# A fused feed-forward, recurrence, feed-forward kernel on 8 cores: gate projections and scans at other places, one product moved into layer one, weight sums all on VectorE, two more plain tiles

## The chip, the cores and the metric

One Trainium2 chip (trn2), 8 cores, each with its own two sequences of the batch of 16; the cores don't talk to each other. The metric is the device time in microseconds of the slowest core. Three runs of the kernel before took 4605.74, 4753.08 and 4896.73 us; their median, 4753.08 us, is its time.

## The reference

```python
# x: (16, 4096, 1024) f32;  w1: (4096, 1024), w2: (1024, 4096), Wa, Wx: (1024, 1024)
def ffn(x):                     # twice: before and after the recurrence
    h = gelu(bitlinear(x, w1, b1))          # exact gelu
    return bitlinear(h, w2, b2)
def bitlinear(x, w, b):
    x = x * rsqrt(mean(x*x) + 1e-5)
    xq = round(x * 127/max|x|) * max|x|/127      # 8-bit activations per token
    wq = clip(round(w / mean|w|), -1, 1) * mean|w|   # ternary weights
    return xq @ wq.T + b
def recurrence(x):
    r, i = sigmoid(x @ Wa.T + ba), sigmoid(x @ Wx.T + bx)
    a = exp(-8 * softplus(-Lam) * r)
    h[t] = a[t] * h[t-1] + sqrt(1 - a*a)[t] * (i * x)[t]
    return h
x = x + 0.5 * ffn(layernorm(x))
x = x + recurrence(layernorm(x))
x = x + 0.5 * ffn(layernorm(x))
```

## The kernel before

Tokens are worked on in tiles of 128. A core has 64 tiles, and each passes the feed-forward twice, so that there are 128 **slots** `j`, one tile each: `plan` (L316) mixes tiles of the first pass with tiles of the second. The recurrence works on groups `t` of 256 tokens; its work is cut into steps (`recur`, L967) laid into three slots in a row for each group. With `R0 = 9`, slot j has stage (j - 9) % 3.

**Setup** (`weights`, L142) loads w1 and w2, finds their mean absolute values, rounds and clips them to ternary fp8 numbers and transposes them. It ends near 172 us. w2T, the ternary w2, stays in SBUF until slot 6; then its room is used by the recurrence.

**One slot**, as the loop at L1089 writes it, in the order of the queues (each engine works strictly in the order in which the loop issues to it, and waits only for semaphores):

- layer one in four parts: `mm1(cur, p)` is 16 matmuls of 512 columns on TensorE into one of two PSUM buffers `f_pm`; `evict1` is the VectorE pass that takes it to SBUF (L498) and the gelu on ScalarE (L504); `gmax` is the VectorE maximum (L509).
- between the parts, for the next tile: `stats`, `centre` (VectorE L426, then the GpSimd addition L429) and `quant1` (from L434 on). For the tile before: `t2`, two times 8 transposes on TensorE into one of two PSUM buffers `aux` and a copy of 1.85 us on ScalarE (L469).
- then `scale2`, and rows 0 to 3 (`row`, L1073), between which the next tile's `t1` (4 transposes), the quantising of the hidden layer (`quant2`), squares on ScalarE and the steps of the recurrence stand.

**Layer two.** For two tiles (slots 2K and 2K+1) it takes seven products of 16 matmuls in place of eight (a scheme of the Strassen kind): `product(K, o)` for o = 0 to 6. Their right sides are sums of quarters of w2, kept in DRAM as `w2x` and read back piece by piece, 512 KB each, into four buffers `w_x`; a piece is asked for when the piece four earlier is used up (`w2_piece`, L621). Their left sides are sums that VectorE makes (`sum1` to `sum4`, L694 to L716) in even slots. Slots with even j hold three products, odd ones four. The first pair (slots 1 and 2) is worked plainly from w2T (`mm2`, L568), 64 matmuls a tile.

**Making w2x**: `w2_plain` stores three quarters as they are; `w2_sum` (L737) makes four sums, in four parts each (u = j = 0 to 3), steps 0 and 2 on VectorE, steps 1 and 3 on GpSimd; `w2_stage` stores them. All four steps of a part stand at the end of the slot, and the first `product` is in slot 4. In slots 1 to 4, `gate_piece` (L780) transposes the gate weights.

**The recurrence of a group**: stage 0 brings in the normalised input by transposes (`g_tr_in`); stage 1 has the gates of channels 0 to 3 and stage 2 those of channels 4 to 7 (`g_gate`: 16 matmuls of 256 columns into `aux`, two tanh on ScalarE, the gate's weights loaded into one of three buffers). Half 0's `g_decay` and `g_root` (exp, square, square root on ScalarE, L901 to L915) stand at the end of stage 1, half 1's at the end of stage 2. `g_gated` (VectorE L918), `g_product` (L925) and `g_scan` (L929, four scans of 256 and a copy) follow in layer one of the next slot; `g_tr_out` (L944) is four transposes of the result into `aux` and an addition by VectorE (L956), which frees the buffer. The two for half 1 stand in stage 0 of the next group: the first straight after layer one (at = -1), the second after row 0 and `t1` (at = 0).

**`aux`** has two buffers, taken strictly in turn (`next_aux`, L383) by `t2`, `t1`, `g_tr_in`, `g_gate` and `g_tr_out`. Whoever writes one waits for the reader of its last content.

All loads and stores go through SyncE's queue, in order.

Of the kernel before, what the change touches and what calls it, by code (L numbers as in the profile page):

```python
# [88 lines left out]
def build_program(B_core=2, S_seq=4096):  # L89
# [34 lines left out]
    with ExitStack() as top:  # L124
# [189 lines left out]
        R0 = 9  # L314

# [22 lines left out]
        def stream_phase():  # L338
# [13 lines left out]
            with ExitStack() as ph:  # L352
# [11 lines left out]
                with nc.Block("stream") as blk:  # L364
# [250 lines left out]
                    n_pieces = 14 * (len(tiles) // 2 - 1)  # L615
# [12 lines left out]
                    def product(K, o):  # L628
# [7 lines left out]
                        for half in range(2):  # L636
                            i = 14 * (K - 1) + 2 * o + half
# [99 lines left out]
                    def w2_sum(u, step):  # L737
# [5 lines left out]
                        eng = ("vector", "gpsimd", "vector", "gpsimd")[step]  # L743
# [5 lines left out]
                            eng, lambda e: e.tensor_tensor(  # L749
# [217 lines left out]
                    def recur(j, at):  # L967
# [12 lines left out]
                        if stage == 0:  # L980
                            if 1 <= t <= NG:
                                if at == -3:
                                    g_gated(t - 1, 1)
                                    g_product(t - 1, 1)
                                elif at == -2:
                                    g_scan(t - 1, 1)
                                elif at in (-1, 0):
                                    g_tr_out(t - 1, at + 1, 1)
# [11 lines left out]
                        elif stage == 1:  # L1000
                            if live and -1 <= at < 3:
                                g_gate(t, at + 1)
                            if live and at == 3:
# [6 lines left out]
                        elif live:  # L1010
                            if at == -3:
                                g_gated(t, 0)
                                g_product(t, 0)
                            elif at == -2:
                                g_scan(t, 0)
                            elif at < 3:
                                g_gate(t, at + 5)
                                if at in (1, 2):
                                    g_tr_out(t, at - 1, 0)
                            else:  # L1020
# [52 lines left out]
                    def row(j, r):  # L1073

                        K = j // 2 - 1
                        if j in (1, 2):
                            mm2(j - 1, r)
                        elif j >= 4 and (j % 2 == 1 or r < 3):
                            product(K, r + 3 * (j % 2))

                    def row_out(j, r):
                        K = j // 2 - 1
                        if j in (1, 2):
                            if r == 3:
                                outp(j - 1)
                        elif j >= 4 and (j % 2 == 1 or r < 3):
                            product_out(K, r + 3 * (j % 2))

                    for j in range(len(slots) + 2):  # L1089
                        cur, nxt, pre = tile(j), tile(j + 1), tile(j - 1)  # L1090
                        K = j // 2 - 1
                        even = j % 2 == 0 and j >= 4
                        order = (1, 0) if j % 2 == 0 else (0, 1)
                        if j == 6:
                            sch.fence([gate_prep[k] for k in ("cast15", "tr15", "wg14", "wg15")]
                                      + [prep["x2"], prep["x3"], prep["plain"], T[1]["mm2"]])
# [130 lines left out]
```

How the kernel before makes its waits and increments, by code:

```python
            def body(engine, ops=ops):  # L73
                passed = {}
                for waits, fn, sem, n in ops:
                    for s, v in waits:
                        if passed.get(s, 0) >= v:
                            continue
                        engine.wait_ge(self.sems[s], v)
                        passed[s] = v
                    ins = fn(engine)
                    if n:
                        ins.then_inc(self.sems[sem], n)
# [1096 lines left out]
            @blk.sync  # L1180
            def _(q):
                for s in ("sOA", "sOB", "sGO"):
                    q.wait_ge(sch.sems[s], sch.count[s])
                q.nop()
```

## Time and profile before

| what | before |
|---|---|
| median of 3 runs | 4753.08 us (4605.74 to 4896.73) |
| the profiled execution | 4604.44 us |
| its span on the slowest core | 4602.9 us; the others 4574.7 to 4602.9 |
| busy | TensorE 4191.7 us (91%), VectorE 3457.2 (75%), ScalarE 2778.1 (60%), GpSimd 935.6 (20%) |
| granted TensorE clock, mean | 0.971 |
| DMA | 864.66 MB, 188 GB/s, 54.8% of the 16 engines; a piece of `w_x` or a gate's weights (512 KB) lands 5.4 us after its issue |
| eviction of a product (L668), `g_norm` (L843) | 0.75 and 0.80 us, mean |

A row of a time order has the start in us from the span's beginning, the duration in us, the engine, the line of the kernel and the instruction, output<-input with the shapes, and how many there were; in brackets is how long the engine was idle before it and what ended that. The end of a matmul is modelled and reaches into the next one. A granted clock of 1 is 2.4 GHz, of 0.5 it is 1.2 GHz.

### The profile page before, as it was taken

Reading aid. Unit: us, or ns where it says so; the run is one execution under the profiler, and the core shown is the slowest. Engines: PE = TensorE matmul, PEld = TensorE weight load, DVE = VectorE, ACT = ScalarE, POOL = GpSimd, SP = SyncE. Lnnn points to the kernel's source line nnn. Section 1 sums busy time; section 2 is a strip of 40 time slices with the busy share of each in tenths; the row PEclk is TensorE's granted clock in tenths of the full one; section 3 lists DMA queues with packets and bytes.
Section 4 is the critical chain, followed back from the end, with each engine's and each line's share of the span. In section 5 each row is a group of like instructions: output and inputs, shape, how many; then the busy total and the mean of one; then the engine's idle time right before and its main releaser. Section 6 shows DMA issues by size and latency. Waiting matters only on the chain.

```text
span 4602.9 us, 72256 instructions; the slowest of 8 cores (4574.7 to 4602.9 us)
## 1 busy us (share of the span) xinstructions
PE 4191.7 (91%) x23447; PEld 2225.5 (48%) x23447; DVE 3457.2 (75%) x4616; ACT 2778.1 (60%) x3464; POOL 935.6 (20%) x1549
## 2 busy tenths in 40 slices
PE   1679999999999999999999999999999999999999
PEld 0334544555555555555554555555555555444444
DVE  4777787777778777777787777778777777777775
ACT  4544666666666666666666666666666666555443
POOL 0232121212212122111121112212212111222221
PEclk9989999999999999999999999999999999999999
DMA  9455545555555555556555555555555555455545
GB/s 286 158 181 166 203 170 188 175 200 200 190 188 190 202 198 175 188 189 209 192 175 188 176 194 203 192 188 195 203 197 170 193 182 192 149 178 179 169 166 179
DMA packets 243090, 864.66 MB, mean 188 GB/s; under 512 B 25608, under 2 KB 31904, under 8 KB 242592
## 3 DMA queue, kind: packets, MB, share of 16 engines
q1 hardware_dynamic: 242720, 860.04, 54.8%
q8 instruction: 193, 3.16, 0.3%
q14 instruction: 177, 1.45, 0.1%
HBM read 747.75 MB, written 112.20 MB: 187 GB/s over the span
## 4 chain that ended last, share of the span: by engine, by line
PE 76%; DVE 10%; DMA 7%; issue 5%; SPq 1%; ACT 1%; POOL 0%; DVEq 0%; ACTq 0%; POOLq 0%
PE f_po L641 31%; PE f_pm L485 30%; PE aux L876 10%; DMA w_x<-w2x 6%; PE aux L462 2%; DVE f_h L498 2%; DVE w2T L934 2%; DVE f_col L509 2%; PE aux L948 2%; DMA p_ring<-L_ffn_w 2%; SPq L62 1%; DVE f_col L434 1%; DVE w2T L918 1%; PE aux L852 1%; PE f_po L574 1%
## 5 line engine op out<-in xcount | busy, mean ns | idle before, releaser
L485 PE MATMUL f_pm<-w1T,f_q1T 128*128 128x512 fp8e4 x8192 | 1840.0, 380 | 15.6 <-DVE f_h L498 10.6
L485 PEld LDWEIGHTS f_pm<-w1T,f_q1T 128*128 128x128 f16 x8192 | 792.9, 98 | 918.4 <-issue 29.3
L641 PE MATMUL f_po<-w_x,f_A 128*128 128x512 fp8e4 x5040 | 1182.7, 390 | 54.1 <-DMA w_x<-w2x 51.1
L504 ACT ACTIVATE f_h<-f_h 128x1024 f32<-128x1024 f32 x512 | 537.7, 1056 | 820.6 <-DVE f_h L498 811.5
L498 DVE SCALAR_TENSOR_TENSOR f_h<-f_pm,f_col,f_b1c 128x1024 f32<-128x1024 f32 x512 | 654.8, 1279 | 252.4 <-PE f_pm L485 247.2
L668 DVE SCALAR_TENSOR_TENSOR f_xb<-f_po,f_col,f_xb 128x512 f32<-128x512 f32 x504 | 376.7, 749 | 619.7 <-PE f_po L641 592.4
L641 PEld LDWEIGHTS f_po<-w_x,f_A 128*128 128x128 f16 x5040 | 501.4, 100 | 632.1 <-issue 127.2
L509 DVE TENSOR_REDUCE f_col<-f_h 128x1 f32<-128x1024 f32 x512 | 616.3, 1214 | 14.5 <-ACT f_h L504 5.3
L516 ACT ACTIVATE f_sqj<-f_h 128x1024 bf16<-128x1024 f32 x512 | 540.6, 1056 | 26.6 <-ACT f_sqj L516 0.7
L429 POOL TENSOR_TENSOR f_xb<-f_xb,f_b2c 128x1024 f32<-128x1024 f32 x128 | 302.2, 2361 | 1053.0 <-DVE f_xb L426 1011.6
L641 PE MATMUL f_po<-w_x,f_s 128*128 128x512 fp8e4 x2016 | 493.6, 401 | 10.3 <-DMA w_x<-w2x 8.7
L876 PE MATMUL aux<-w2T,g_w 128*128 128x256 bf16 x4096 | 488.9, 273 | 0.3 <-ACT w2T L890 0.3
L469 ACT CAST f_A<-aux 128x2048 f16<-128x2048 int8 x256 | 472.8, 1847 | 16.5 <-PE aux L462 16.5
L876 PEld LDWEIGHTS aux<-w2T,g_w 128*128 128x128 bf16 x4096 | 397.6, 98 | 87.4 <-issue 0.4
L545 POOL TENSOR_TENSOR f_col<-f_col 128x2 f32<-128x2 f32 x128 | 36.9, 289 | 1798.4 <-ACT f_sqj L516 1798.4
L469 ACT CAST f_q1T<-aux 128x1024 f16<-128x1024 int8 x128 | 129.6, 1012 | 392.4 <-PE aux L462 392.4
L641 PEld LDWEIGHTS f_po<-w_x,f_s 128*128 128x128 f16 x2016 | 206.9, 103 | 257.3 <-issue 63.0
L886 ACT ACTIVATE w2T<-aux,ba_h 128x256 f32<-128x256 f32 x256 | 120.6, 471 | 329.1 <-PE aux L876 329.1
L539 DVE TENSOR_SCALAR f_q<-f_h,f_col 128x1024 int8<-128x1024 f32 x448 | 305.8, 742 | 0.1
L948 PE MATMUL aux<-ident_f,w2T 128*128 128x128 f32 x512 | 92.6, 312 | 177.5 <-DVE w2T L934 166.7
L462 PEld LDWEIGHTS aux<-ident_b,f_q 128*128 128x128 bf16 x2560 | 175.2, 98 | 96.2 <-issue 6.1
L462 PE MATMUL aux<-ident_b,f_q 128*128 128x128 bf16 x2560 | 205.6, 219 | 6.0 <-ACT f_q L443 6.0
(103 smaller groups left out, 3718.5 us busy)
## 6 DMA issues: line engine op xcount, KB each, us to landing
w_x<-w2x SPq DMA_DIRECT2D x882, 512.0 KB, 5.4
g_w<-wg SPq DMA_DIRECT2D x256, 512.0 KB, 5.4
p_ring<-L_ffn_w SPq DMA_DIRECT2D x64, 512.0 KB, 16.1
f_xb<-L_attn_x SPq DMA_DIRECT2D x64, 512.0 KB, 6.2
xs<-f_xb SPq DMA_DIRECT2D x64, 512.0 KB, 5.9
g_xg<-xs SPq DMA_DIRECT2D x32, 1024.0 KB, 8.7
xs<-g_xg SPq DMA_DIRECT2D x32, 1024.0 KB, 7.4
f_xb<-xs SPq DMA_DIRECT2D x64, 512.0 KB, 5.7
```

Of the source, the lines that this page charges most:

```text
L429: tj["xb2"] = put("gpsimd", lambda g: g.tensor_tensor(x[:], x[:], b2c[:], op=ALU.add), waits=tok_b2 + [tj["xc"]])
L462: a = put("tensor", lambda t, c=c: t.transpose(out[:, c * 128:(c + 1) * 128], words[:, c * 128:(c + 1) * 128], ident_b[:]), waits=(waits_p ...
L469: ev = put("scalar", lambda s: s.copy(dst.rearrange("p (c i t) -> p c i t", i=2, t=128), pair), waits=[a] + waits_act)
L485: a = put("tensor", lambda t, k=k, hf=hf, o=o: t.matmul(pm[i][:, hf * 512:(hf + 1) * 512], q1T[:, k * 128:(k + 1) * 128], w1T[:, o:o + 512 ...
L498: ev = put("vector", lambda v: v.scalar_tensor_tensor(hg[:, sl], pm[i][:], col(n, C1), b1c[:, sl], op0=ALU.mult, op1=ALU.add), waits=[tj[" ...
L504: tj["gelu%d" % p] = put("scalar", lambda s: s.activation(hg[:, sl], hg[:, sl], AF.Gelu), waits=[ev])
L509: T[n]["gm"] = put("vector", lambda v: v.reduce_max(col(n, GM + p), hg[:, sl], axis=AX.X, apply_absolute_value=True), waits=[T[n]["gelu%d" ...
L516: tj["sq"] = put("scalar", lambda s: s.activation(sqj[:], hg[:, sl], AF.Square, accum_out=col(n, SQ + p)), waits=[tj["gelu%d" % p], tj.get ...
L539: T[n]["q2"] = T[n]["q2_%d" % (p // 2)] = put("vector", lambda v: v.tensor_single_scalar(q2[:, sl], hg[:, sl], col(n, S2), op=ALU.mult), w ...
L641: a = put("tensor", lambda t, k=k, c=c, w=w: t.matmul(po[:, bank * 512:(bank + 1) * 512], lhs[:, k * 128:(k + 1) * 128], w[:, c * 512:(c + ...
L668: "vector", lambda v: v.scalar_tensor_tensor(x[:, sl], po[:, bank * 512:(bank + 1) * 512], col(n, C2), x[:, sl], op0=ALU.mult, op1=ALU.add),
L876: a = put("tensor", lambda q, h=h, k=k: q.matmul(aux[i][:, h * TW:(h + 1) * TW], w[:, h * D + k * 128:h * D + (k + 1) * 128], xnB[:, k * T ...
```

## The change

There are five edits.

1. `PLAIN = 4`: four tiles (slots 1 to 4) instead of two are worked plainly from w2T; products begin in slot 6.
2. `w2_sum` runs on VectorE alone, one step after each row of slots 0 to 3; the stores follow row 3. The first loads of `w_x` are asked for at the end of slot 4.
3. Product 3 of a pair, the one from `sum1`, moves in odd slots from row 0 to the middle of layer one, between parts 1 and 2; the other three are rows 0 to 2. There is no row 3 after slot 5.
4. Two gates stand right behind layer one (at = -1), the third at 0 and the fourth at 1; `g_decay` and `g_root` move from 3 to 2, ahead of row 3's place.
5. `g_gated` moves to the very start of the slot (at = -5, ahead of `evict1(cur, 0)`), `g_product` behind `evict1(cur, 1)` (-4), `g_scan` behind `quant1` (-3), ahead of `gmax(cur, 0)` and `evict1(cur, 2)`. The places of `g_tr_out` for half 1 stay.

```diff
+        PLAIN = 4
...
-                    n_pieces = 14 * (len(tiles) // 2 - 1)
+                    n_pieces = 14 * (len(tiles) // 2 - PLAIN // 2)
...
-                            i = 14 * (K - 1) + 2 * o + half
+                            i = 14 * (K - PLAIN // 2) + 2 * o + half
...
-                        eng = ("vector", "gpsimd", "vector", "gpsimd")[step]
...
-                            eng, lambda e: e.tensor_tensor(
+                            "vector", lambda v: v.tensor_tensor(
...
                         if stage == 0:
                             if 1 <= t <= NG:
-                                if at == -3:
+                                if at == -5:
                                     g_gated(t - 1, 1)
+                                elif at == -4:
                                     g_product(t - 1, 1)
-                                elif at == -2:
+                                elif at == -3:
                                     g_scan(t - 1, 1)
...
                         elif stage == 1:
-                            if live and -1 <= at < 3:
-                                g_gate(t, at + 1)
-                            if live and at == 3:
+                            if live and at == -1:
+                                g_gate(t, 0)
+                                g_gate(t, 1)
+                            if live and at in (0, 1):
+                                g_gate(t, at + 2)
+                            if live and at == 2:
                                 g_decay(t, 0)
                                 g_root(t, 0)
...
                         elif live:
-                            if at == -3:
+                            if at == -5:
                                 g_gated(t, 0)
+                            elif at == -4:
                                 g_product(t, 0)
-                            elif at == -2:
+                            elif at == -3:
                                 g_scan(t, 0)
-                            elif at < 3:
-                                g_gate(t, at + 5)
-                                if at in (1, 2):
-                                    g_tr_out(t, at - 1, 0)
-                            else:
+                            elif at == -1:
+                                g_gate(t, 4)
+                                g_gate(t, 5)
+                            elif at == 0:
+                                g_gate(t, 6)
+                            elif at == 1:
+                                g_gate(t, 7)
+                                g_tr_out(t, 0, 0)
+                            elif at == 2:
+                                g_tr_out(t, 1, 0)
                                 g_decay(t, 1)
                                 g_root(t, 1)
...
-                        if j in (1, 2):
+                        if 1 <= j <= PLAIN:
                             mm2(j - 1, r)
-                        elif j >= 4 and (j % 2 == 1 or r < 3):
-                            product(K, r + 3 * (j % 2))
+                        elif j >= PLAIN + 2 and r < 3:
+                            product(j // 2 - 1, r + 4 * (j % 2))
...
+                        if j < 4:
+                            w2_sum(j, r)
+                            if r == 3:
+                                for step in range(4):
+                                    w2_stage(j, step)
...
+                        recur(j, -5)
                         if cur is not None:
                             mm1(cur, 0)
                             evict1(cur, 0)
...
                             mm1(cur, 1)
                             evict1(cur, 1)
+                        recur(j, -4)
                         if pre is not None:
                             t2(pre, order[0])
                         if nxt is not None:
                             quant1(nxt)
+                        recur(j, -3)
+                        if odd:
+                            product(K, 3)
                         if cur is not None:
                             gmax(cur, 0)
                             mm1(cur, 2)
-                            recur(j, -3)
                             evict1(cur, 2)
+                        if odd:
+                            product_out(K, 3)
+                        if cur is not None:
                             gmax(cur, 1)
                         if pre is not None:
                             t2(pre, order[1])
                         if cur is not None:
                             mm1(cur, 3)
                             evict1(cur, 3)
-                            recur(j, -2)
                             gmax(cur, 2)
                             gmax(cur, 3)
                             scale2(cur)
                         recur(j, -1)
...
-                        if j < 4:
-                            for step in range(4):
-                                w2_sum(j, step)
-                            for step in range(4):
-                                w2_stage(j, step)
-                        if j == 3:
+                        if j == 4:
                             wx_ready += [sch.tok(x) for x in XSEM + ("sXP",)]
```

Here `even` and `odd` are true from slot 6 on, for even and odd j.

## Rows read from the trace of the kernel before

**Rows 1.** Waits of TensorE, whole span (total us, times, longest us).

```profile
PE aux L948 <- DVE w2T L934: 166.7, 30, 5.9
PE f_po L641 <- DMA w_x<-w2x: 59.8, 46, 5.7
```

**Rows 2.** TensorE from 2081.75 (start, duration us, instructions, [idle before]).

```profile
2081.75 7.07 PE L485 MATMUL f_pm<-w1T,f_q1T 128*128 128x512 fp8e4 x32
2093.01 3.62 PE L485 MATMUL f_pm<-w1T,f_q1T 128*128 128x512 fp8e4 x16
2102.15 1.09 PE L948 MATMUL aux<-ident_f,w2T 128*128 128x128 f32 x4 [5.53 <-DVE w2T L934]
2103.03 5.67 PE L641 MATMUL f_po<-w_x,f_A 128*128 128x512 fp8e4 x16
2132.56 1.91 PE L876 MATMUL aux<-w2T,g_w 128*128 128x256 bf16 x16
```

**Rows 3.** VectorE in time order, same slot, and the sums at its end.

```profile
2085.61 1.28 DVE L498 SCALAR_TENSOR_TENSOR f_h<-f_pm,f_col,f_b1c 128x1024 f32<-128x1024 f32 x1 [1.98 <-PE f_pm L485]
2090.44 1.21 DVE L434 TENSOR_REDUCE f_col<-f_xb 128x1 f32<-128x1024 f32 x1
2092.11 1.22 DVE L509 TENSOR_REDUCE f_col<-f_h 128x1 f32<-128x1024 f32 x1
2093.25 1.22 DVE L918 SCALAR_TENSOR_TENSOR w2T<-w2T 128x1024 f32<-128x1024 f32 x1
2094.57 1.23 DVE L925 TENSOR_TENSOR w2T<-w2T 128x1024 f32<-128x1024 f32 x1
2095.71 1.28 DVE L498 SCALAR_TENSOR_TENSOR f_h<-f_pm,f_col,f_b1c 128x1024 f32<-128x1024 f32 x1
2099.22 2.67 DVE L934 TENSOR_TENSOR_SCAN w2T<-w2T,carry 128x256 f32<-128x256 f32 x4
2105.18 0.69 DVE L956 TENSOR_TENSOR g_xg<-aux,g_xg 128x512 f32<-128x512 f32 x1
2117.98 1.22 DVE L708 TENSOR_TENSOR f_A<-f_s,f_A 128x2048 f16<-128x2048 f16 x1
```

**Rows 4.** ScalarE in time order, same slot.

```profile
2084.93 1.06 ACT L914 ACTIVATE w2T<-w2T 128x1024 f32<-128x1024 f32 x1
2097.08 1.06 ACT L504 ACTIVATE f_h<-f_h 128x1024 f32<-128x1024 f32 x1 [2.60 <-DVE f_h L498]
2098.05 1.85 ACT L469 CAST f_A<-aux 128x2048 f16<-128x2048 int8 x1
2099.79 1.06 ACT L504 ACTIVATE f_h<-f_h 128x1024 f32<-128x1024 f32 x1
```

**Rows 5.** GpSimd in time order: the same slot, and slot 1's end.

```profile
2089.48 2.37 POOL L429 TENSOR_TENSOR f_xb<-f_xb,f_b2c 128x1024 f32<-128x1024 f32 x1 [11.27 <-DVE f_xb L426]
...
236.22 3.83 POOL L749 TENSOR_TENSOR w_x<-w2T 128x2048 fp8e4<-128x2048 fp8e4 x1 [5.75 <-DVE w_x L749]
```

**Rows 6.** VectorE in time order, around 236 us.

```profile
233.79 2.28 DVE L749 TENSOR_TENSOR w_x<-w2T 128x2048 fp8e4<-128x2048 fp8e4 x1
236.25 5.94 DVE L749 TENSOR_TENSOR w_x<-w_x,w2T 128x2048 fp8e4<-128x2048 fp8e4 x1 [0.17 <-DVE w_x L749]
```

**Rows 7.** TensorE in time order, around the first slots' waits.

```profile
243.53 5.26 PE L485 MATMUL f_pm<-w1T,f_q1T 128*128 128x512 fp8e4 x16 [3.92 <-DVE f_h L498]
254.95 3.61 PE L574 MATMUL f_po<-w2T,f_A 128*128 128x512 fp8e4 x16 [2.26 <-ACT f_A L469]
324.53 5.72 PE L641 MATMUL f_po<-w_x,f_A 128*128 128x512 fp8e4 x16 [5.74 <-DMA w_x<-w2x]
```

**Rows 8.** Busy time by engine in a stretch, with TensorE granted clock (PEclk).

```profile
172.00:377.00 205.00, 164.85 (x856) 78.41 (x857) 151.04 (x168) 98.72 (x112) 72.25 (x74) 0.92 0.50 162
```

**Rows 9.** Waits of TensorE between 640 and 4100, then 4100 and 4603 us.

```profile
PE f_po L641 <- DMA w_x<-w2x: 29.4, 21, 2.7
...
PE f_po L641 <- DMA w_x<-w2x: 13.9, 16, 1.7
```

More of the change, by code:

```diff
@@ L1073, in row @@
                     def row(j, r):
-                        K = j // 2 - 1
-                        if j in (1, 2):
+                        if 1 <= j <= PLAIN:
                             mm2(j - 1, r)
-                        elif j >= 4 and (j % 2 == 1 or r < 3):
-                            product(K, r + 3 * (j % 2))
+                        elif j >= PLAIN + 2 and r < 3:
+                            product(j // 2 - 1, r + 4 * (j % 2))
                     def row_out(j, r):
-                        K = j // 2 - 1
-                        if j in (1, 2):
+                        if 1 <= j <= PLAIN:
                             if r == 3:
                                 outp(j - 1)
-                        elif j >= 4 and (j % 2 == 1 or r < 3):
-                            product_out(K, r + 3 * (j % 2))
+                        elif j >= PLAIN + 2 and r < 3:
+                            product_out(j // 2 - 1, r + 4 * (j % 2))
+                        if j < 4:
[3 more added lines that the diff above has]
+                                    w2_stage(j, step)
                     for j in range(len(slots) + 2):
@@ L1091, in stream_phase @@
                         K = j // 2 - 1
-                        even = j % 2 == 0 and j >= 4
+                        even = j % 2 == 0 and j >= PLAIN + 2
+                        odd = j % 2 == 1 and j >= PLAIN + 2
                         order = (1, 0) if j % 2 == 0 else (0, 1)
@@ L1095, in stream_phase @@
                             sch.fence([gate_prep[k] for k in ("cast15", "tr15", "wg14", "wg15")]
-                                      + [prep["x2"], prep["x3"], prep["plain"], T[1]["mm2"]])
-                        if cur is None and even:
+                                      + [prep["x2"], prep["x3"], prep["plain"],
+                                         T[PLAIN - 1]["mm2"]])
+                        drain = cur is None and even
+                        if drain:
                             for r in range(2):
@@ L1129, in stream_phase @@
                         recur(j, -1)
-                        if cur is not None or not even:
+                        if not drain:
                             row(j, 0)
@@ L1145, in stream_phase @@
                             sum3(K)
-                        if cur is not None or not even:
+                        if not drain:
                             row(j, 1)
```

## The prediction

> **What bounds the kernel.** I read the waits of TensorE first, then its instructions in order of time, then the other engines in the same slot. TensorE is busy 91% of the span and in most slots has no gap at all. Its largest wait, 166.7 us in 30 places, is `g_tr_out` waiting for the scans; the pieces `w_x` cost 59.8 us in 46 [rows 1]. Below, S is a slot's first matmul; the slot at S = 2081.75 is even, with stage 0. Layer one ends, and TensorE stands 5.53 us until the scans of half 1 are through, because they stand behind `evict1(cur, 3)`. What follows is slow: the four transposes take 1.09 us and the next product 5.67 where 16 such matmuls take 3.62 [rows 2], the granted clock being at its lower level. That wait costs about 5.5 + 0.5 + 2.05 = 8.1 us, so a pair of groups (six slots: one even and one odd slot of each stage) pays 16.1, and 16 such pairs pay 258 us. This is what edits 4 and 5 aim at. The question is whether VectorE and `aux` let it go.
>
> **The new place of the scans (edit 5).** TensorE without gaps: 16 matmuls are 7.07 - 3.62 = 3.45 us, a gate 1.91 less the same 0.17 of overlap, 1.74 [rows 2]; with two `t2` of about 0.45, layer one ends at S + 14.7, and in an odd slot, which now has a product in its middle, at S + 18.2. VectorE is anchored to TensorE by the first eviction at S + 3.86 (2085.61) and then works without a break. In before, L434 starts at S + 8.69, `gmax` at 10.36, `g_gated` 11.50, `g_product` 12.82, the third eviction at 13.96 [rows 3]. Now `g_gated` lies under TensorE's first part, and `g_product` stands ahead of L434, at S + 8.69. It reads two SBUF tensors while GpSimd's L429 runs, S + 7.73 to 10.10 [rows 5]. No row has these two together, since L925 came 4 us later. The nearest is L749: 5.94 us when a GpSimd L749 had begun just before, against 2.28 for its twin [rows 6]: it waited until GpSimd was done. The price of this collision lies between 0 and 2.37 us; I take 1.4, the end of L429 less the start of `g_product`, as in the L749 row. Then L434 starts at 11.2, the scans at 12.9 (quant1's 1.67 us later), `gmax` at 15.8 (2.67 and a copy) and the third eviction at 16.9, 3.0 us later than in before.
>
> The Trainium skill (SBUF — State Buffer, "Who interferes with whom") says that a VectorE instruction with two SBUF inputs and a GpSimd instruction that reads SBUF exclude each other, the later one waiting for the whole of the first. The L749 rows agree (5.94 us against 2.28). Without that rule the sum below would be 4541 us.
>
> **Who is late next.** `t2`'s second copy on ScalarE stands behind the gelu of part 2, so it starts when the third eviction is through: before, at S + 16.3 until 18.15 [rows 4]; now until 21.1. It holds one `aux` buffer. The gelu of part 3 follows it, then `gmax(cur, 3)` at 22.1, `scale2`, and the addition L956 of the first `g_tr_out` at 24.05 to 24.7, which holds the other. From this:
> - *stage 0, even*: the scans are ready 15.8, TensorE is there at 14.7; `t1` finds `aux` free at 21.3; the second `g_tr_out` starts at 25.0 where without waits it would at 18.8. **6.2 us** in three steps, in place of 5.53.
> - *stage 2, even*: the second of the two gates behind layer one needs the buffer of the `t2` copy: free at 21.3, wanted at 14.7 + 1.74 = 16.45: **4.85 us**. This is new: before, one gate stood there.
> - *odd slots*: TensorE comes 3.45 us later, but VectorE begins the slot with `sum2` and `sum4` (1.22 each [rows 3]) of the even slot before, and `g_gated` now stands ahead of the first eviction. Counted from the end of product 2, with a start after 0.34, an eviction of 0.7, the sums' 2.4, `g_norm`'s 0.75 and `g_gated`'s 1.15: 5.3 against 3.86, shift 1.5, in stage 2; 0.9 in stage 0. Stage 2: free at 22.9, wanted 19.9, **3.0 us**. Stage 0: with product 3's own eviction (0.66) as well, free at 26.0, wanted 22.3, **3.7 us**.
> - *stage 1*: no scan; the copy is through at about S + 15.8 and the second gate comes at 16.45: nothing. The root is done in time: it ended at S + 4.24 in the slot [rows 4] and moves by less than a row of 3.45, to 7.7 at most, ahead of 8.69.
>
> Waits for six slots: 17.75 us, before 11.06. **Clock**: a wait of 2.26 us was followed by full speed (16 matmuls in 3.61), one of 3.92 by 5.26 [rows 7], one of 5.53 by 2.54 us of loss in all. I take 2.5 for the 6.2, 1.9 for the 4.85, 1.7 for the 3.7, and for the 3.0, between 0 and 1.64, the middle, 0.8: 6.9. In all 24.6 against 16.1: +8.5 for six slots, times 16 = **+136 us**.
>
> **Product 3 inside layer one (edit 3).** Same matmuls, and `sum1` and its pieces are long there. Its two pieces are given back earlier, so the four `w_x` buffers refill under layer one. In before the pieces made TensorE wait 29.4 us between 640 and 4100 us, at 2.7 us at the most [rows 9]; the new waits give the loads time as well. I take 20 us of it back (0 to 30). Where products follow each other without gates, behind 3940 us, the waits are short and many (13.9 us in 16 from 4100 on [rows 9]); only odd slots, with four products in a row, can run through four buffers that way, and now none has more than three: I take 15 (8 to 18). SyncE's queue keeps its order of waits; the gate weights, two asked for in quick succession, have about 12 us until their use, against 5.4 for a landing.
>
> **The first slots (edits 1 and 2).** The stretch from slot 0 to slot 6 lasts 205.0 us, of which TensorE is busy 164.9 at 0.92 of the clock [rows 8]. A slot with plain rows and gate pieces is 30.5 us of TensorE. Now: slot 0 19; slot 1 about 42 (VectorE's sums, 4 x 2.28 us in place of two, push its evictions by some 4 us, partly taken out of a wait that was there); slots 2 and 3 about 33.3 each (16 sums cost 36.5 us of VectorE against 25.6 before, but they lie beside the rows; the block ahead of the first eviction, 2.28 + 5.94, which gave the 3.92 us wait [rows 6, 7], is gone); slot 4 31; slot 5, with no layer two, 19.5. Sum 178: **-26 us** (-10 to -35). Two more plain tiles are 16 matmuls more, 3.45 us, contained in this. The wait for the first piece, 5.74 us and its slow product [rows 7], goes, since the pieces are now asked for a slot ahead. Of the 59.8 us of piece waits, 29.4, 13.9 and this 5.7 leave 10.8 for slots 4 to 9 and around 4000 us; I take **-8** for slots 6 to 9 (0 to -10).
>
> **Sum** against the profiled execution: 4604.4 + 136 - 20 - 15 - 26 - 8 = 4671, say **4670 us**, +1.4%. The profiled execution stands 149 us below the median of the three runs shown; I keep to it as the base, and let the range reach up. A difference under 2%, 4512 to 4697, is about what can't be told from no change.
>
> **Rivals.**
> 1. *The wait just goes* (0.12). If the copy and the addition come earlier than I place them, TensorE has no gap in stages 0 and 2: 4604 - 258 - 69 = 4277 us. For: VectorE is idle for a quarter of the span. Against: the idle time lies in stage 1 and late in the slots, and the copy stands behind a later eviction by order.
> 2. *No collision with GpSimd* (0.20). Each of the four waits is 1.4 us shorter: 4.8, 3.45, 1.6 and 2.3, 12.1 in all, with 4.4 of clock 16.5 for six slots, nearly before's 16.1: 4604 + 6 - 69 = 4541. For: L925 always took 1.22 to 1.23 us. Against: it never stood beside L429.
> 3. *Slower: the clock* (0.18). Place: every slot of stages 0 and 2. Price: the 2.54 us that followed the wait of 5.53 [rows 2], after each of the four waits: 17.75 + 10.2 = 27.9 against 16.1, + 189, so 4604 + 189 - 69 = 4724. It decides if waits of 3 to 4 us in quick succession always bring the lower level; 3.92 did, 2.26 didn't.
> 4. *Mine* (0.50): 4600 to 4740.
>
> The change does what it says on every engine; the only part that may not act is the shorter time for pieces.
>
> **Range**: 4520 to 4790. Below it takes in most of rival 2, above it rival 3 and part of the spread of the runs shown; rival 1 is left out. Faster by over 2%: rival 1 and a third of rival 2, 0.18. Slower by over 2%: most of rival 3 and the upper quarter of mine, 0.28. Within: 0.54.
>
> **What would show it.** Right: no wait of `g_tr_out` beyond about 1 us for the scans, but waits of TensorE for ScalarE's L469 (gate at L876 and `t1`) and for VectorE's L956, 3 to 6 us in every slot of stages 0 and 2; L925 at 2.6 us; third evictions at S + 17; no piece waits in the tail; slot 6 starting near 351 us instead of 377. Wrong: L925 at 1.23 (rival 2); waits under 1 us at gates and `g_tr_out` (rival 1); a mean granted clock clearly under 0.97 (rival 3); or a VectorE backlog that makes `mm1` wait for evictions, which I have at nothing because `f_pm` is next needed in the following slot.

## The result and the profile after

The changed kernel's profiled execution took 4652.14 us against 4604.44, +1.0%. Against runs of the kernel before on the same chip (4603.36 us at best) the ratio is 1.011, 95% interval 1.0065 to 1.0152: slower, by less than the 2% that the prediction called hard to tell from no change. The four runs took 4652.14, 4656.47, 4883.84 and 4968.73 us; in the two long ones the cores of one die show a lower granted clock, as happens in some executions of every version here, so that ratios and not medians are compared below. The span is 4650.6 us on the slowest core, the mean granted clock 0.964 (0.971 before), TensorE is busy 4226.9 us and VectorE 3528.9.

What makes TensorE wait has changed hands. Waits of TensorE over the whole span, changed kernel: total us, times, longest us. Lines between 316 and 740 have a number one higher than before (L470 was L469, L642 was L641); L876 to L956 keep theirs.

```profile
PE aux L876 <- ACT f_A L470: 110.7, 33, 4.8
PE aux L948 <- DVE g_xg L956: 109.2, 32, 3.6
PE aux L463 <- ACT f_A L470: 21.2, 16, 1.3
PE aux L948 <- DVE w2T L934: 11.3, 15, 0.8
PE f_po L642 <- DMA w_x<-w2x: 9.2, 16, 1.4
```

[Rows 1] had 166.7 us in 30 for the scans and 59.8 in 46 for pieces. The scans' wait is down to 11.3, and 241 us of waits for the copy and the addition that free an `aux` buffer have come (110.7 + 109.2 + 21.2), none of which were there. All of the 9.2 us for pieces lies behind 3985 us.

The same even slot of stage 0 as in [rows 2], TensorE in time order (start, duration us, instructions, idle before):

```profile
2103.22 0.63 PE L948 MATMUL aux<-ident_f,w2T 128*128 128x128 f32 x4 [0.78 <-DVE w2T L934]
...
2108.63 0.38 PE L463 MATMUL aux<-ident_b,f_q 128*128 128x128 bf16 x4 [1.33 <-ACT f_A L470]
2112.33 1.09 PE L948 MATMUL aux<-ident_f,w2T 128*128 128x128 f32 x4 [3.32 <-DVE g_xg L956]
2113.21 5.53 PE L642 MATMUL f_po<-w_x,f_A 128*128 128x512 fp8e4 x16
```

One wait of 5.53 us has become three, 0.78, 1.33 and 3.32, in all 5.43; and the slow product behind them, at the lower of the two clock levels for most of its time, is still there (5.53 us for what takes 3.62).

The next slots of stages 2 and 0, TensorE in time order: even stage 2 (layer one from 2159.50), odd stage 0 (from 2199.53), odd stage 2 (from 2268.53).

```profile
2180.48 3.57 PE L876 MATMUL aux<-w2T,g_w 128*128 128x256 bf16 x16 [4.37 <-ACT f_A L470]
2183.85 4.35 PE L642 MATMUL f_po<-w_x,f_A 128*128 128x512 fp8e4 x16
...
2225.45 0.63 PE L948 MATMUL aux<-ident_f,w2T 128*128 128x128 f32 x4 [3.48 <-DVE g_xg L956]
2225.91 5.30 PE L642 MATMUL f_po<-w_x,f_s 128*128 128x512 fp8e4 x16
...
2290.80 3.28 PE L876 MATMUL aux<-w2T,g_w 128*128 128x256 bf16 x16 [2.20 <-ACT f_A L470]
2293.88 3.96 PE L642 MATMUL f_po<-w_x,f_A 128*128 128x512 fp8e4 x16
```

The reason stands in the other queues of the even stage-2 slot. VectorE, then GpSimd, then ScalarE, in time order:

```profile
2168.12 2.47 DVE L925 TENSOR_TENSOR w2T<-w2T 128x1024 f32<-128x1024 f32 x1
2172.16 2.66 DVE L934 TENSOR_TENSOR_SCAN w2T<-w2T,carry 128x256 f32<-128x256 f32 x4
2176.16 1.28 DVE L499 SCALAR_TENSOR_TENSOR f_h<-f_pm,f_col,f_b1c 128x1024 f32<-128x1024 f32 x1
...
2167.15 2.35 POOL L430 TENSOR_TENSOR f_xb<-f_xb,f_b2c 128x1024 f32<-128x1024 f32 x1 [3.87 <-DVE f_xb L427]
...
2177.53 1.06 ACT L505 ACTIVATE f_h<-f_h 128x1024 f32<-128x1024 f32 x1 [4.05 <-DVE f_h L499]
2178.49 1.85 ACT L470 CAST f_A<-aux 128x2048 f16<-128x2048 int8 x1
2180.24 1.06 ACT L505 ACTIVATE f_h<-f_h 128x1024 f32<-128x1024 f32 x1
```

The product L925 takes 2.47 us where it took 1.23 [rows 3], since GpSimd's L430 runs at the time. The third eviction starts 16.66 us into the slot (S + 13.96 before), ScalarE stands 4.05 us for it, and its copy, behind the gelu, frees TensorE's buffer at 2180.3; the gate starts at 2180.48, 4.37 us after TensorE had come to it.

Busy time by engine in four stretches (from the setup's end to slot 6, to slot 10, to the drain, to the end), with the granted clock as the third number from the end:

```profile
172.00:348.00 176.00, 157.41 (x873) 76.32 (x874) 144.78 (x162) 95.14 (x105) 45.87 (x60) 0.98 0.50 156
348.00:460.00 112.00, 111.87 (x576) 53.22 (x577) 92.10 (x125) 63.72 (x75) 27.85 (x48) 0.98 0.50 157
460.00:3996.00 3536.00, 3284.92 (x18504) 1787.40 (x18502) 2701.46 (x3563) 2218.30 (x2804) 755.76 (x1180) 0.95 0.56 185
3996.00:4651.00 655.00, 633.37 (x3249) 297.12 (x3246) 490.30 (x637) 322.92 (x363) 138.12 (x243) 1.00 0.52 176
```

Slot 6 starts at 347.96 (377.18 before), slot 10 at 460.07 (497.46), the first slot after the last scans at 4009.67 (3955.02). So 37.4 us are gained until slot 10, 92.0 are lost in the 96 slots behind it, and 7.0 are gained in the tail: together +47.7, the difference of the spans (4650.6 and 4602.9).

### The profile page after: what moved, and what is told of

It is laid out like the page before. It is cut to its first block, busy times and chain, and to the rows that moved or that the text cites. A ratio compares the mean times of both kernels' runs of the same rounds, so it can differ in the third digit from the quotient of the medians.

```text
span 4650.6 us, 72145 instructions; the slowest of 8 cores (4639.2 to 4650.6 us)
## 1 busy us (share of the span) xinstructions
PE 4226.9 (91%) x23463; PEld 2238.2 (48%) x23463; DVE 3528.9 (76%) x4614; ACT 2789.5 (60%) x3464; POOL 974.2 (21%) x1541
## 4 chain that ended last, share of the span: by engine, by line
PE 67%; DVE 17%; issue 7%; DMA 4%; ACT 3%; SPq 1%; DVEq 0%; POOL 0%; ACTq 0%; POOLq 0%
PE f_pm L486 28%; PE f_po L642 26%; PE aux L876 9%; DVE f_h L499 3%; DVE w2T L934 2%; DVE w2T L925 2%; PE aux L463 2%; DMA w_x<-w2x 2%; ACT f_A L470 2%; DMA p_ring<-L_ffn_w 2%; PE aux L948 1%; DVE f_col L510 1%; PE aux L852 1%; DVE f_q L540 1%; SPq L62 1%
## 5 line engine op out<-in xcount | busy, mean ns | idle before, releaser
L642 PE MATMUL f_po<-w_x,f_A 128*128 128x512 fp8e4 x4960 | 1165.4, 390 | 11.2 <-DMA w_x<-w2x 8.9
L642 PEld LDWEIGHTS f_po<-w_x,f_A 128*128 128x128 f16 x4960 | 496.6, 101 | 582.1 <-issue 78.8
L876 PE MATMUL aux<-w2T,g_w 128*128 128x256 bf16 x4096 | 534.5, 290 | 110.7 <-ACT f_A L470 110.7
L876 PEld LDWEIGHTS aux<-w2T,g_w 128*128 128x128 bf16 x4096 | 417.9, 103 | 213.4 <-issue 119.0
L546 POOL TENSOR_TENSOR f_col<-f_col 128x2 f32<-128x2 f32 x128 | 60.4, 472 | 2033.4 <-ACT f_sqj L517 2033.4
L470 ACT CAST f_A<-aux 128x2048 f16<-128x2048 int8 x256 | 472.7, 1847 | 12.8 <-PE aux L463 12.8
L642 PE MATMUL f_po<-w_x,f_s 128*128 128x512 fp8e4 x1984 | 475.6, 396 | 1.9 <-DVE f_xb L669 1.4
L430 POOL TENSOR_TENSOR f_xb<-f_xb,f_b2c 128x1024 f32<-128x1024 f32 x128 | 301.8, 2358 | 718.2 <-DVE f_xb L427 676.8
L642 PEld LDWEIGHTS f_po<-w_x,f_s 128*128 128x128 f16 x1984 | 197.4, 101 | 229.4 <-issue 40.3
L470 ACT CAST f_q1T<-aux 128x1024 f16<-128x1024 int8 x128 | 129.0, 1008 | 231.0 <-PE aux L463 231.0
L463 PE MATMUL aux<-ident_b,f_q 128*128 128x128 bf16 x2560 | 205.7, 220 | 27.6 <-ACT f_A L470 21.2
L863 ACT CAST w2T<-w2T 128x512 bf16<-128x512 f32 x128 | 77.8, 618 | 199.8 <-DVE w2T L860 199.8
```

What stands on the lines that cost most here:

```text
L430: tj["xb2"] = put("gpsimd", lambda g: g.tensor_tensor(x[:], x[:], b2c[:], op=ALU.add), waits=tok_b2 + [tj["xc"]])
L463: a = put("tensor", lambda t, c=c: t.transpose(out[:, c * 128:(c + 1) * 128], words[:, c * 128:(c + 1) * 128], ident_b[:]), waits=(waits_p ...
L470: ev = put("scalar", lambda s: s.copy(dst.rearrange("p (c i t) -> p c i t", i=2, t=128), pair), waits=[a] + waits_act)
L642: a = put("tensor", lambda t, k=k, c=c, w=w: t.matmul(po[:, bank * 512:(bank + 1) * 512], lhs[:, k * 128:(k + 1) * 128], w[:, c * 512:(c + ...
L876: a = put("tensor", lambda q, h=h, k=k: q.matmul(aux[i][:, h * TW:(h + 1) * TW], w[:, h * D + k * 128:h * D + (k + 1) * 128], xnB[:, k * T ...
```

## The experiments

Each kernel was timed beside the kernel before on the same chip, and ratios are to that. The changed kernel was timed on one chip only; where microseconds are counted from its 4652.1, lowest times are compared, and the lowest of the kernel before lay between 4602.1 and 4604.4 on all chips. In the time orders and waits below the columns are as above.

**Edits 4 and 5 taken back, and edits 4 and 5 alone.** In the first, `recur` and its places in layer one are those of before, with edits 1 to 3 kept (the lines below are the places alone; the gates, `g_decay`, `g_gated`, `g_product` and `g_scan` go back inside `recur` too); the second is the converse.

```diff
 (first, against the changed kernel)
-                        recur(j, -5)
...
-                        recur(j, -4)
...
-                        recur(j, -3)
...
                             mm1(cur, 2)
+                            recur(j, -3)
...
                             evict1(cur, 3)
+                            recur(j, -2)
```

> The changed kernel with edits 4 and 5 undone: gates, decay, gated, product and scans stand where they stood before; the plain tiles, the sums on VectorE and product 3 inside layer one stay. My theory (the loss is made by the earlier scans, through the aux buffers; the other edits gain): the first slots keep 37 us, the tail 7 us and the piece waits of 29 us stay away, while g_tr_out waits for the scans again, 5.5 us in even stage 0 slots and some 4.6 in odd ones: 4520 to 4550 us, ratio to before 0.985. Rival (product 3 in layer one or the plain tiles cost the time): at or above 4604 us, ratio 1.00 to 1.02.

> The kernel before with edits 4 and 5 alone. My theory: the waits for the t2 copy and for the first g_tr_out's addition are there in all slots of stages 0 and 2, and larger in odd slots by up to the 3.45 us that product 3 no longer gives: waits of about 22 us for six slots in place of 11, 4750 to 4850 us, ratio 1.03 to 1.05. Rival (the scans' place gains as meant, and something else in the change loses more): under 4604 us, about 4450.

Measured: without edits 4 and 5 0.976 [0.973, 0.979], 4493.7 us at best, further down than I had it; with them alone 1.045 [1.042, 1.048], 4812.5, inside the range given. Waits of TensorE in the first, with those of an even and an odd stage-0 slot, then in the second:

```profile
PE aux L948 <- DVE w2T L934: 136.6, 28, 5.6
PE aux L948 <- DVE carry L941: 19.4, 4, 5.6
PE f_po L642 <- DMA w_x<-w2x: 17.5, 21, 3.3
...
2039.69 1.09 PE L948 MATMUL aux<-ident_f,w2T 128*128 128x128 f32 x4 [5.53 <-DVE w2T L934]
...
2147.26 0.63 PE L948 MATMUL aux<-ident_f,w2T 128*128 128x128 f32 x4 [4.23 <-DVE w2T L934]
```

```profile
PE aux L876 <- ACT f_A L469: 164.6, 32, 6.2
PE aux L948 <- DVE g_xg L956: 106.5, 32, 3.7
PE aux L462 <- ACT f_A L469: 42.4, 32, 1.3
PE aux L948 <- DVE w2T L934: 32.8, 28, 2.0
```

So the change is two changes of opposite sign: edits 1 to 3 take about 108 us away, edits 4 and 5 give 158 back on top of them (4493.7 to 4652.1) and 208 on the kernel before (4604 to 4812). Without product 3 amid layer one TensorE reaches the gates of odd slots a row earlier, and the waits for the copy are 164.6 us instead of 110.7.

No run has edit 4 without edit 5, so how the copy's wait divides between them is not shown. An estimate for the even stage-2 slot, from rows: the second gate is wanted at S + 16.6. With edit 4 alone the copy would be through at S + 18.15, as [rows 4] has it, which leaves about 1.6 us of wait. With edit 5 alone the gate would be wanted a row and `t1` later, at about S + 20.3, against a buffer free at S + 21.0: under 1 us. The 4.37 us would then need both edits.

**Edits 1 and 2 alone**, to split the 108 us: product 3 goes back to row 0 of odd slots.

```diff
 (against the kernel without edits 4 and 5)
-                        elif j >= PLAIN + 2 and r < 3:
-                            product(j // 2 - 1, r + 4 * (j % 2))
+                        elif j >= PLAIN + 2 and (j % 2 == 1 or r < 3):
+                            product(j // 2 - 1, r + 3 * (j % 2))
...
-                        if odd:
-                            product(K, 3)
```

`product_out` goes with it.

> The kernel before with edits 1 and 2 alone (four plain tiles, weight sums on VectorE row by row). With edits 1 to 3 it was 4494 us against 4602, so 108 us less. Mine: edits 1 and 2 give 26 to 37 us until slot 10 and nothing behind it, 4565 to 4575, and the rest, some 70 us, is edit 3's: waits for pieces (about 44 us) and the stretch of odd slots in which layer one becomes 3.45 us longer, so that VectorE's scans are late by less. Rival: edit 3 gives no more than the waits for pieces, and edits 1 and 2 give more than the first slots show: 4530 to 4540.

Measured: 4582.09 us at best against 4604.33, -0.5% (no interval), 7 us above my range. TensorE's waits:

```profile
PE aux L948 <- DVE w2T L934: 166.2, 30, 5.9
PE f_po L642 <- DMA w_x<-w2x: 56.2, 40, 5.9
```

To the scans' 166.2 come 11.1 us in 2 for L941. Of the pieces' waits 35.3 us in 22 lie between 640 and 3990. So edit 3 is worth about 88 us (4582.1 to 4493.7): waits for scans 177.3 to 156.0, pieces 56.2 to 17.5, 60 us; the other 28 go with the clock (0.972 in the one, 0.98 in the other; TensorE's busy time falls from 4187.0 to 4161.0 us). The rival is out.

**The product behind `quant1`.** This takes the collision away: GpSimd's L430 is done by then. Apart from the exchange of `g_product` and `quant1` in VectorE's order nothing changes.

```diff
-                        recur(j, -4)
                         if pre is not None:
                             t2(pre, order[0])
                         if nxt is not None:
                             quant1(nxt)
+                        recur(j, -4)
                         recur(j, -3)
```

> The changed kernel with g_product behind quant1 instead of ahead of it, so that it no longer starts while GpSimd's addition L430 runs; nothing else differs. My theory: L925 takes 1.22 us instead of 2.47, the third eviction comes 1.2 us sooner, each of the four waits of six slots gets about 1.2 us shorter and some stretches of slow clock go: 4540 to 4580 us, ratio 0.985 to 0.995. Rival (the length of L925 does not reach TensorE): 4650 us, ratio 1.01.

Measured: 0.988 [0.985, 0.991] of before, 4551.3 us at best, in the range expected and 101 us under the changed kernel. L925 in the changed kernel, then in this one (min/median/max ns), and this one's waits:

```profile
L925 DVE TENSOR_TENSOR w2T<-w2T x64: 2466/2474/2484, 505.2 to 3984.3; 128x1024 f32<-128x1024 f32 x64
```

```profile
L925 DVE TENSOR_TENSOR w2T<-w2T x64: 1224/1225/1226, 512.1 to 3885.9; 128x1024 f32<-128x1024 f32 x64
...
PE aux L948 <- DVE g_xg L956: 93.1, 32, 3.7
PE aux L876 <- ACT f_A L470: 78.9, 33, 3.7
```

64 instructions lose 1.25 us each, 80 us of VectorE, and 101 us of the kernel's time hang on them. By the Trainium skill (SBUF — State Buffer, "Who interferes with whom") a VectorE instruction with two SBUF inputs contends with a GpSimd instruction that reads SBUF; the trace agrees, 64 of 64 at 2.47 us beside L430 and 64 of 64 at 1.225 away from it.

**The copy ahead of the gelu.** The second `t2` is issued before `evict1(cur, 2)`.

```diff
                             mm1(cur, 2)
+                        if pre is not None:
+                            t2(pre, order[1])
+                        if cur is not None:
                             evict1(cur, 2)
...
                             gmax(cur, 1)
-                        if pre is not None:
-                            t2(pre, order[1])
```

> The changed kernel with the second t2 issued ahead of evict1(cur, 2), so that on ScalarE its copy stands ahead of the gelu of part 2; the orders on TensorE and VectorE stay. My theory (the gate and t1 wait for the aux buffer that this copy holds): the waits for L470 go (132 us in 49 places in the profile), g_tr_out still waits for the addition L956, up to 5 us: about 4480 us (4450 to 4530), ratio 0.973. Rival (ScalarE or VectorE is itself the limit, the wait only changes its name): 4620 to 4660 us.

Measured: 4493.0 us at best, 0.976 of before's best 4602.1 (no interval), in my range. Of the waits for L470 0.3 us is left, 13.6 us in 32 for ScalarE's L890 have come, and the largest is:

```profile
PE aux L948 <- DVE g_xg L956: 127.8, 32, 4.4
```

The waits for the addition grew by 18.6 us: TensorE gets there earlier, the addition does not.

**The first addition of half 1 earlier**, alone on the changed kernel.

```diff
-                                elif at in (-1, 0):
-                                    g_tr_out(t - 1, at + 1, 1)
+                                elif at == -2:
+                                    g_tr_out(t - 1, 0, 1)
+                                elif at == 0:
+                                    g_tr_out(t - 1, 1, 1)
...
                             mm1(cur, 3)
+                        recur(j, -2)
+                        if cur is not None:
                             evict1(cur, 3)
```

> The changed kernel with the first g_tr_out of half 1 between mm1(cur, 3) and evict1(cur, 3), nothing else. Mine: the waits for L956 (109.2 us in 32) go, but the scans are through only at about S + 14.8, so that some waits for L934 stay, and the buffer of the t2 copy L470 is still free only at S + 20: the waits for L470 stay at 130 us or more, since in stage 0 too the next user of that buffer now meets it. Time 4480 to 4560. Rival 1: the addition is the whole cost in stage 0: 4650 - 109 - 70 of clock, about 4470 or less, with waits for L470 unchanged at 132. Rival 2: the copy just takes its place in all 32 slots: 4620 to 4650.

Measured: 0.985 [0.983, 0.987], 4537.2 us at best, in my range; both rivals are out.

```profile
PE aux L876 <- ACT f_A L470: 110.9, 33, 4.7
PE aux L852 <- DVE g_xn L843: 36.9, 16, 2.6
...
PE aux L852 <- DVE g_xg L956: 6.9, 17, 0.6
```

The 109.2 us at L948 are gone, the copy's waits are as they were, and 44 us have turned up at L852, the transposes of `g_tr_in`. That they had been hidden behind the larger wait is my reading.

**The moves together.** First the product and the copy; then the addition as well.

> The two moves together: g_product behind quant1 and the second t2 with its copy ahead of the gelu of part 2. Mine: L925 back at 1.22 us, no waits for the copy L470 at all, and what is left are the waits of g_tr_out for the addition L956 (127.8 us in 32 with the copy moved alone), each about 1 us shorter since VectorE no longer loses 1.24 us at L925: some 95 us in 32. From 4493 us (copy moved alone) that is 32 x 1 us with its share of clock, 40 to 60 us less: 4430 to 4455 us. Rival: the additions depend on TensorE's own pace and not on L925, so that the waits stay at 128 us: 4490.

> As the run with both moves, and the first g_tr_out of half 1 goes between mm1(cur, 3) and evict1(cur, 3), so that its addition L956 stands ahead of the last eviction, gmax and scale2. Mine: the waits for L956 shrink from some 95 us to under 20, with them the lower clock behind them, and stage-0 slots run at TensorE's pace: 4280 to 4340 us. Rival: VectorE, which has about 30 us of work in an even slot of stage 0 against TensorE's 28, becomes the bound there and TensorE waits for evictions or sums instead: 4380 to 4430.

Measured: 0.960 [0.957, 0.963], 4422.7 us at best, and 0.941 [0.939, 0.943], 4333.9 at best, inside the 4280 to 4340 expected. Waits of the first, then of the second with TensorE of its even stage-0 slot:

```profile
PE aux L948 <- DVE g_xg L956: 109.7, 32, 4.7
```

```profile
PE aux L852 <- DVE g_xn L843: 36.5, 16, 2.6
PE aux L852 <- DVE g_xg L956: 20.0, 16, 1.6
...
1962.28 0.60 PE L948 MATMUL aux<-ident_f,w2T 128*128 128x128 f32 x4
1962.72 3.62 PE L642 MATMUL f_po<-w_x,f_A 128*128 128x512 fp8e4 x16
...
1978.54 1.06 PE L852 MATMUL aux<-ident_f,g_xn 128*128 128x128 f32 x8 [2.28 <-DVE g_xn L843]
1979.44 5.78 PE L486 MATMUL f_pm<-w1T,f_q1T 128*128 128x512 fp8e4 x26
```

With the product and the copy moved the addition's waits came down by 18 us only, not by 33, but the time by more than I had (to 4422.7, expected 4430 to 4455). With the addition moved as well row 0 of the slot takes 3.62 us, behind no wait. One by one the three moves take 101, 159 and 115 us off the changed kernel, 375; together 318, so part of what they save is the same.

**Another way to remove the large wait**: edits 1 to 3 only, scans where before has them, and the two `g_tr_out` of half 1 one place later (the store of the group, `g_store`, moves from 0 to 1 with them).

```diff
 (against the kernel without edits 4 and 5)
-                                elif at in (-1, 0):
-                                    g_tr_out(t - 1, at + 1, 1)
+                                elif at in (0, 1):
+                                    g_tr_out(t - 1, at, 1)
```

> Edits 1 to 3 as in the run without edits 4 and 5 (scans where the kernel before has them), and the two g_tr_out of half 1 one place later: behind row 0 and t1, and behind row 1. TensorE then has a row of 3.45 us and t1 between the end of layer one and its need of the scans. There the waits for L934 and L941 were 156 us in 32, 5.3 us in an even slot and 4.2 in an odd one. Mine: 1.4 us at the most stays in an even slot, under 1 in an odd one, the total falls to 20 to 40 us and the lower clock behind it goes: 4494 - 125 - 60 = about 4310 (4290 to 4350). So the large wait of the kernel before could be had without moving the scans. Rival: VectorE's backlog in the even slots of stage 0 turns up at the g_tr_in transposes, with over 60 us of waits at L852: 4380 or more.

Measured: 0.971 [0.965, 0.976], 4466.0 us at best, 156 above my number. The time is the rival's; TensorE's waits, and two rows of an odd stage-0 slot:

```profile
PE aux L852 <- DVE g_xg L956: 101.4, 35, 4.4
PE aux L948 <- DVE w2T L934: 32.4, 28, 1.9
...
2141.34 0.63 PE L852 MATMUL aux<-ident_f,g_xn 128*128 128x128 f32 x4 [1.96 <-DVE g_xg L956]
2141.81 5.30 PE L642 MATMUL f_po<-w_x,f_A 128*128 128x512 fp8e4 x16
```

The scans' wait fell from 156.0 to 34.9 (32.4 at L934 and 2.5 at L941), as I had it, but the additions, now later in VectorE's queue, release their buffers late for the next user, `g_tr_in`. A later consumer doesn't help when what it releases is wanted just behind.

**Two more steps from the best version.** `sum1` and `sum3` of even slots go behind `recur(j, 1)`; then the second `g_tr_out` of half 1 goes to at = -1 too.

```diff
-                        if even:
-                            sum1(K)
-                            sum3(K)
...
                         recur(j, 1)
+                        if even:
+                            sum1(K)
+                            sum3(K)
...
 (second step)
-                                elif at == 0:
+                                elif at == -1:
                                     g_tr_out(t - 1, 1, 1)
```

> The version with the copy ahead of the gelu, the product behind quant1 and the first addition of half 1 ahead of the last eviction (4332 us), and sum1 and sum3 of even slots go behind the work of place 1, so that the copies L860 and g_norm L843 of stage 0 don't stand behind them. There TensorE waited 36.5 us in 16 for L843 and 20.0 in 16 for L956. Mine: the first goes, the second stays, and 36 us with some lower clock come off: 4285 to 4305. Rival: TensorE waits somewhere else for the same backlog of VectorE (row 2's eviction, the sums, or mm1's evictions in the next slot): 4320 to 4335.

> The version with sum1 and sum3 behind the copies (undisturbed cores 4273 to 4290 us), and the second g_tr_out of half 1 goes from behind row 0 to straight behind layer one, so that its addition stands ahead of the eviction of row 0. What was left there is 19.9 us in 16 of the second pair of g_tr_in waiting for L956. Mine: they go, 15 to 20 us come off, undisturbed cores at 4255 to 4275. Rival: the transposes of the second g_tr_out then need the buffer of the addition L956 or of the t2 copy before it is free, and TensorE waits at L948 for 1 us or more in each stage-0 slot: 4285 to 4320.

Measured: the first 4309.8 us at best against 4603.6 (-6.4%, no interval; its cores with a granted clock of 0.997 or 0.998 have spans of 4273 to 4290, where those of the version without it had 4310 to 4337 at 0.996 to 0.998); the waits for L843 are gone, and 19.9 us in 16 for L956 stay. The second 0.931 [0.928, 0.933], 4292.6 at best, with spans of 4273 to 4296 at that clock. What is left:

```profile
PE aux L852 <- DVE g_xg L956: 17.7, 16, 1.4
PE f_po L642 <- DMA w_x<-w2x: 16.1, 22, 2.3
...
1957.27 0.69 DVE L956 TENSOR_TENSOR g_xg<-aux,g_xg 128x512 f32<-128x512 f32 x1
1958.11 1.06 PE L852 MATMUL aux<-ident_f,g_xn 128*128 128x128 f32 x8 [1.07 <-DVE g_xg L956]
```

The second step did nothing that can be seen, against my expectation, and the rival's waits at L948 did not come either: ahead of `row_out` the addition still stands behind the last eviction, the maxima and `scale2`, which end at 1957.3. This last version is the best that was run, 6.9% under the kernel before and 7.7% under the changed one (4292.6 to 4652.1).

## Why the prediction was right in its mechanism, and which of its steps failed

The mechanism came as forecast, and counted from the profiled execution of before the size was near: +66 us forecast (4604.4 to 4670), +48 measured (4604.44 to 4652.14). These steps failed:

- **The base.** The forecast is a time, 4670 us, and it was built on the profiled execution ("I keep to it as the base") while the time of the kernel before stood as 4753.08. Beside that figure 4670 says 1.7% faster; the change is slower, 1.011 [1.0065, 1.0152], and the medians of four runs each are 4679.41 before and 4770.16 after, 100 us above the forecast. What had been worked out was a difference, and only the difference held.
- **The waits, sized too long.** 17.75 us for six slots; the slots shown have 15.5, all waits of this kind in the span 253.2 us, 15.8 for six slots, against 177.6 and 11.1 before. That is +76 us where +107 was forecast.
- **The clock, sized too small.** 6.9 us of loss for six slots; the slots shown have 8.2. In the steady part TensorE's busy time grew by 41.9 us for the same 18504 matmuls (3243.0 us between 497 and 3943, 3284.9 between 460 and 3996), where +29 was forecast.
- **Edit 3, priced at its pieces alone.** 20 + 15 = 35 us. What it does for the scans' wait of odd slots, and for the clock behind it, stood at nothing; with the scans in their old place it was worth about 88. So edits 1 to 3 took 108 us away where the prediction has 69, and edits 4 and 5 gave 158 back where it has 136 for the steady part. These two misses, 39 and 22, have opposite signs; that the total came within 18 us is in part luck.

Term by term:

- **The large wait goes, two buffers come free too late in its place.** Right. Even stage 0 5.4 us (predicted 6.2), even stage 2 4.4 (4.85), odd stage 0 3.5 (3.7), odd stage 2 2.2 in the slot shown and 2.4 in others (3.0). For odd stage 0 the terms as written, 25.0 + 0.9 + 0.66, give 26.6 and not 26.0; the trace has the buffer free at S + 25.9. Moving the copy took away its waits, moving the addition those for it: the two causes are shown one by one.
- **The collision**, priced at 1.4 us from the single L749 row [rows 6], was 1.25 in each of 64. The third eviction came at S + 16.7 (16.9). The overlap was real and worth 101 us in all; rival 2 had put 4541 on a kernel without it, and the kernel without it took 4551.
- **Clock.** The losses behind the four waits were 2.40 us (0.49 + 1.91), 2.39 (1.66 + 0.73), 1.7 and 1.71 (1.37 + 0.34), where 2.5, 1.9, 1.7 and 0.8 had been taken. The furthest off is the 0.8, the middle between nothing and 1.64: a wait of 2.20 already brought 1.7, though 2.26 had brought nothing in [rows 7]. Rival 3 had 2.5 behind each of them; two of four did about that, which is not enough for its 4724.
- **Pieces.** 20 us in the steady part were too careful: all 29.4 [rows 9] went. In the tail 15 were too much: 13.9 became 9.2 at L642, and the span of that part shrank by 7.0. The sign "no piece waits in the tail" did not come.
- **The steady part**: +75.6 us of waits, +41.9 of clock and -29.4 of pieces make 88.1; 92.0 was measured, so 4 us stay unassigned. Predicted was 136 - 20 = 116.
- **The first slots.** -29.2 to slot 6 (predicted -26) and -8.2 to slot 10 (-8). All 16 sums took 2.28 us on VectorE; the 5.94 of [rows 6] does not occur.
- **Rival 1** put 4277 on a kernel in which the wait just goes. The changed kernel is not that one; with three more moves it took 4333.9 us, with two more 4292.6. What the rival left out are the buffers' releases.

## What to carry to other kernels

When a wait on an in-order engine is taken away by moving work forward, list the instructions that the moved work now stands in front of, and for each the buffer that it releases and who takes it next; with two buffers taken in turn, whoever takes the buffer next waits for a copy or addition that comes later (here 241 us in all). Issue the releasing instruction first: the copy and the addition put ahead, together with the product moved out of GpSimd's way, turned +1.1% into -5.9%. Moving the consumer later is the weaker tool, since the wait turned up again at the next user of the buffer (101.4 us, where 121 of the scans' 156 had gone).

## What the runs showed of the hardware

- A VectorE product of two SBUF tensors beside a GpSimd addition: 2.47 us in 64 of 64, with the GpSimd addition at its usual 2.35; 1.225 in 64 of 64 once apart. The whole price falls on the instruction that comes second: VectorE's began at 2168.12, GpSimd's at 2167.15.
- Waits of the same length cost TensorE very different clock. 2.20 us ahead of a gate was followed by 3.28 us where 1.91 is usual and by 3.96 where 3.62 is (1.7 us lost); 1.96 us between transposes by 5.30 (1.7 lost); 2.28 us ahead of transposes, directly behind a row of products, by 1.06 for 8 transposes and 5.78 for 26 matmuls, nothing lost. Even the same wait of 5.53 us in the kernel before was followed by products of 5.7 and of 6.1 us (at 2103.03 and 2208.01). What decides it was not tried.
- The granted mean clock rises with the waits gone: 0.964 in the changed kernel, 0.982 with the addition moved, 0.988 with product and copy, 0.997 with all three. From the changed kernel to the best version TensorE's busy time falls from 4226.9 to 4095.5 us for the same 23463 matmuls, so that 131 of the 356 us saved in the span are clock.
